# One run of probability products per attention group instead of two, on one Trainium2 core

## The chip, the cores and the metric

The kernel runs on one core of a Trainium2 chip. The metric is the device time of one execution in microseconds (us), taken as the median over several runs. A run is called no different when it lies within 0.2% of the other kernel's time.

## The reference

The reference is an attention layer followed by a small mixture-of-experts layer, for 8 batches of 512 tokens with 512 features:

```python
x = x + attention(layernorm(x), ctx)     # 16 heads of 32, causal mask, softmax
x = x + experts(layernorm(x))            # 8 experts, for each output the two best of 8 logits
```

Only attention is touched by the change. There, with `q = norm(x) Wq`, `k, v = ctx Wkv`, the output of a head is `softmax(q k' / sqrt(32), causal) v`, and the heads' outputs are projected with `Wout` and added to `x`.

## The kernel before

**Groups and steps.** Attention takes the first 615 us or so. A group is four heads of one batch; there are 4 groups a batch (`c` = 0 to 3) and 32 in all (`n`). The loop over a group has 8 steps (`v` = 0 to 7). In step `v` the kernel makes transposed, shifted scores for key block `v // 2` (128 keys) and one pair of the four heads. Key block `kb` holds 512, 384, 256 or 128 columns of queries (causal), so steps 0 and 1 are wide and 6 and 7 narrow.

**Who does what in a step.** TensorE runs two matmuls of `shifted_scores` (L705) into the one PSUM tile `e_ps`. ScalarE takes their exponential into `pT[kb]` (L1095). TensorE may start the next step's L705 only when that exponential has ended. GpSimd then zeroes the masked triangle (`hide_future`, L1836) and, from step 2 on, adds the probabilities of the later key blocks into `acc` (`add`, L1828 and L1823), which is what the sums of the softmax are made from.

**Work for the next group.** The shift of the scores is minus the maximum of each row. TensorE makes the unshifted scores of the group after, three steps ahead (`scores`, L672, in four units of two heads by turns: two PSUM banks, one for each head). VectorE takes their maxima (L1390 and, where masks are added by a matmul, L1384); a bank's next score waits for the maximum of its last. In step 5 TensorE turns the maxima (`turn_maxima`, L687); ScalarE (`hi_shift`, L1020) and VectorE (`lo_shift`, L1399) split them in two parts, and SyncE copies both parts by DMA into two rows of `qk_st` (`rows`, L380, parts `nm_h` and `nm_l`). The next group's first L705 waits for both copies:

```python
if v == 0:
    pe.wait_ge(s["rows_in"], (n + 1) * (16 * SHIFT_ROWS))
```

**Fillers.** The rest of TensorE's work in the steps is put there by tables: queries three groups ahead in steps 0, 2, 3, 4 (`QUERY`), keys in step 5 or 6, values (c = 0 only, steps 0, 2, 3, 4), transposes of tokens (c = 0, steps 6 and 7, `turn_tokens`), and the output projection of the batch before (`project`, 16 steps of a batch: c = 1 steps 0 to 3, 6, 7; c = 2 steps 0, 1, 3 to 6; c = 3 steps 0 to 3). Queries, keys, values and projections are three matmuls of 512 columns each (L261, L262, L263).

**The products with probabilities.** `values_of` (L721) multiplies `v` by `pT[kb]`; `first_sums` (L733) and `other_sums` (L741) multiply ones by `pT[0]` and `acc`. These are matmuls with 32 weight columns, four side by side in the array, while everything else uses all 128 columns (or 16 in L687). The products of key blocks 0 and 1 and the first sums run in step 7 of their own group, those of key blocks 2 and 3 and the other sums in step 1 of the next. In step 2 ScalarE begins the inverse of the sums. The exponential of step 0 of the next group writes `pT[0]` and waits for the products that read it:

```python
if some(n):
    act.wait_ge(s["pv"], (n - 1) * QB + kb + 1)
    act.wait_ge(s["added"], (n - 1) * ADDS + max(v - 1, v % 2 + 1))
```

The last group has a routine of its own (`last_group`), so 31 groups use the code that changes.

Of the kernel before, what the change touches and what calls it, by code (L numbers as in the profile page):

```python
# [27 lines left out]
KC = H // P  # L28
QB = S // P
# [16 lines left out]
def build(nc, x, ctxT, wqT, wkvT, woT, routerT, router_b, expertT, expert_b, out):  # L46
    ctx = ExitStack()
    with ctx:
        def sem(name):
            return ctx.enter_context(nc.semaphore(name))  # L50
# [166 lines left out]
        s = {n: sem(n) for n in names}  # L217

        def some(value):

            return not isinstance(value, int) or value > 0
# [52 lines left out]
        def block_of(v):  # L274

            return QB - 1 - v // 2

        TURN = 5
        LAST = 7
        QUERY = {0: 0, 2: 1, 3: 2, 4: 3}  # L280
        VALUE = {0: 0, 2: 1, 3: 2, 4: 3}
        SUMMED = 1
        STATISTICS = ((2, 0), (2, 1), (3, 0), (3, 1))
        NORMALISED = ((2, 7), (3, 1), (3, 3), (3, 7))
        LAST_GROUP = {3: 0, 5: 1, 7: 2}
# [33 lines left out]
        def out_block(c, v, last):  # L319

            for i, (c0, v0) in enumerate(OUT_FIRST_LAST if last else OUT_FIRST):
                chunk = (c - c0) * UNITS + v - v0
                if 0 <= chunk < KC:
                    return i, chunk
            return None
# [283 lines left out]
        def _(pe):  # L609

            def freed(task, k):
                for name in {"Q": ("q_hi", "q_lo"), "K": ("k_hi", "k_lo"), "V": ("v_ok",),
                             "LNT": ("xT_hi", "xT_lo"), "WO": ("x1_ok",)}[task]:
                    pe.wait_ge(s[name], k + 1)

            def norm_turn(g, i, bank):

                pe.wait_ge(s["xn_ok"], g + 1)
                for k in range(KC):  # L620
                    mm = pe.transpose(j_ps[bank][:, k * P:(k + 1) * P], xt[:, i, k * P:(k + 1) * P], ident[:])
                mm.then_inc(s["xT_mm"], 1)
# [36 lines left out]
            def scores(n, c, v, heads=(0, 1), mask=False):  # L659

                u = n * UNITS + v
                i, pair = block_of(v), v % 2
                w = (i + 1) * P
                if v < 2 and 0 in heads:

                    pe.wait_ge(s[f"stacked{pair}"], (n + 1) * (16 * STACK_DMAS))
                for j in heads:
                    hh = 2 * pair + j

                    if some(2 * u - 1):  # L670
                        pe.wait_ge(s["negmax"], 2 * u - 1 + j)
                    mm = pe.matmul(s_ps[:, j, 0:w], qk_st[c][0:STACK, 0, hh, i * P:w], qk_st[c][0:STACK, 1, hh, 0:w],  # L672
                                   start=True, stop=not mask)
                    if not mask:
                        mm.then_inc(s["scores"], 1)
                if mask:
                    for j in heads:
                        pe.matmul(s_ps[:, j, i * P:w], ident_r[:], mask_r[:], start=False, stop=True)\
                            .then_inc(s["scores"], 1)
# [32 lines left out]
            def values_of(n, c, b, kb):  # L712

                pe.wait_ge(s["causal"], n * UNITS + 2 * kb + 2)
                pe.wait_ge(s["v_ok"], b * QB + kb + 1)
                if kb == 0:
                    if some(n):
                        pe.wait_ge(s["o_ok"], n)
                for hh in range(HC):
                    h = c * HC + hh  # L720
                    mm = pe.matmul(o_ps[hh * HD:(hh + 1) * HD, kb * P:S], v_sb[:, kb, h * HD:(h + 1) * HD],  # L721
                                   pT[kb][:, hh, :], start=(kb == 0), stop=(kb == QB - 1),
                                   tile_position=(0, hh * HD), skip_group_check=True)
                if kb > 0:
                    mm.then_inc(s["pv"], 1)

            def first_sums(n, turned):

                if turned:
                    pe.wait_ge(s["nm_hi"], n + 2)  # L730
                    pe.wait_ge(s["nm_lo"], n + 2)
                for hh in range(HC):
                    mm = pe.matmul(d_ps[hh * HD:(hh + 1) * HD, 0:P], ones[:], pT[0][:, hh, 0:P],  # L733
                                   start=True, stop=True, tile_position=(0, hh * HD), skip_group_check=True)
                mm.then_inc(s["pv"], 1)

            def other_sums(n):

                pe.wait_ge(s["added"], (n + 1) * ADDS)
                for hh in range(HC):  # L740
                    mm = pe.matmul(d_ps[hh * HD:(hh + 1) * HD, P:S], ones[:], acc[:, hh, :],  # L741
                                   start=True, stop=True, tile_position=(0, hh * HD), skip_group_check=True)
                mm.then_inc(s["summed"], 1)
# [16 lines left out]
                                   skip_group_check=True)  # L760
                mm.then_inc(s["summed" if kb == QB - 1 else "pv"], 1)

            def finish_group(n, c, b):
                values_of(n, c, b, QB - 2)
                values_of(n, c, b, QB - 1)
                other_sums(n)

            pe.wait_ge(s["const_one"], 1)
# [38 lines left out]
            def body(b, first, more, further):  # L807
                last = not more
                held = [("K", b * KC + AHEAD - 1), ("Q", b * KC + AHEAD - 1)]

                def take(bank, task, k):
                    freed(*held[bank])
                    held[bank] = (task, k)

                for c in range(KC):
                    n = b * KC + c
                    ahead = more or c == 0

                    def project(v):
                        i, chunk = out_block(c, v, last)  # L820
                        if chunk == 0:
                            take(0, "WO", (b - 1) * QB + i)
                        project_out(b - 1, i, chunk, 0)

                    def turn_tokens(i):
                        take(1 - i % 2, "LNT", (b + 1) * QB + i)
                        norm_turn((b + 1) * QB + i, i, 1 - i % 2)

                    for v in range(UNITS):
                        out = not first and out_block(c, v, last) is not None  # L830
                        final = last and c == KC - 1
                        shifted_scores(n, c, v, final)
                        g, vv = target(c, v - 1)
                        if not masked((c if v else c - 1) % KC, (v - 1) % UNITS) and (more or c + g < KC):
                            scores(n + g, (c + g) % KC, vv, (1,))
                        if c == 1 and v == 0 and out:
                            project(v)
                        if c == 0 and v in VALUE:
                            take(0, "V", b * QB + VALUE[v])
                            values(VALUE[v])  # L840
                        if v in QUERY and ahead:
                            if QUERY[v] == 0:
                                take(1, "Q", n + AHEAD)
                            queries(n + AHEAD, (c + AHEAD) % KC, QUERY[v])
                        if v == SUMMED and not (first and c == 0):
                            finish_group(n - 1, (c - 1) % KC, b if c else b - 1)
                        if final and v in LAST_GROUP:
                            last_group(LAST_GROUP[v])
                        if v == key_step(c) and ahead:
                            take(key_bank(c), "K", n + AHEAD)  # L850
                            keys((c + AHEAD) % KC, b if c == 0 else b + 1, key_bank(c))
                        if v == LAST and not final:
                            values_of(n, c, b, 0)
                            first_sums(n, more or c < KC - 1)
                            values_of(n, c, b, 1)
                        if c == 0 and more:
                            for i in TURNED.get(v, ()):
                                turn_tokens(i)
                        if out and not (c == 1 and v == 0):
                            project(v)  # L860
                        g, vv = target(c, v)
                        if more or c + g < KC:
                            if masked(c, v):
                                scores(n + g, (c + g) % KC, vv, mask=True)
                            else:
                                scores(n + g, (c + g) % KC, vv, (0,))
                        if v == TURN and (more or c < KC - 1):
                            turn_maxima(n + 1, c + 1)
# [1090 lines left out]
```

## Time and profile before

| | |
|---|---|
| median of 3 runs | 1986.51 us (1984.96 to 1989.05) |
| profiled execution, span | 1984.3 us |
| TensorE matmul (PE) busy | 1910.6 us, 96% of the span |
| VectorE (DVE) busy | 1432.1 us, 72% |
| ScalarE (ACT) busy | 1039.0 us, 52% |
| GpSimd (POOL) busy | 850.5 us, 43% |
| chain that ended last | PE 83%, DVE 7%, DMA 3%, issue 2%, POOL 2%, ACT 2% |

A profile comes from one execution, so sums are made against its span. The busy time of PE is that of modelled ends of pipelined matmuls: what tells how long PE is held is the distance from one start to the next. PEld is the loading of weights, which normally lies under the matmul before.

### The profile page before, as it was taken

The page shows a single profiled execution, that of the slowest core. Times are in us where ns is not written, and L with a number is a line of the kernel's source. Part 1 is how long each engine was busy: PE and PEld are TensorE (multiplying, and loading weights), DVE is VectorE, ACT ScalarE, POOL GpSimd, SP SyncE. Part 2 cuts the span into 40 slices and gives each one's busy share as a digit, 9 for nine tenths or more (in the row PEclk, how much of TensorE's full clock was granted, in tenths as well). Part 3 has the DMA queues.
Part 4 walks back from the last instruction along what each step waited for, and adds up shares of the span by engine and source line. Part 5 has one row for each costly group of instructions (what it writes and reads, how often), then busy time and mean ns, then how long its engine had stood idle before and what let it go on. Part 6 is the DMA issues. An engine that isn't in the chain of part 4 may idle for free.

```text
span 1984.3 us, 30426 instructions
## 1 busy us (share of the span) xinstructions
PE 1910.6 (96%) x9772; PEld 1514.7 (76%) x9772; DVE 1432.1 (72%) x2840; ACT 1039.0 (52%) x2062; POOL 850.5 (43%) x1016
## 2 busy tenths in 40 slices
PE   4899999999998999999999999999999999999999
PEld 3666766777765788888888888778888888888887
DVE  5667667767668658787888888477777777777732
ACT  2566566566554347877777787533443333344400
POOL 5577777777674135456445435102321111232100
PEclk8999999999999999999999999999999999999999
DMA  5454555455466468787856555822232222223111
GB/s 166 121 125 130 137 144 128 124 149 134 108 166 229 159 229 274 231 271 221 254 203 217 190 186 196 313 85 79 94 118 85 80 95 85 80 86 124 49 42 33
DMA packets 103693, 294.54 MB, mean 148 GB/s; under 512 B 13777, under 2 KB 14801, under 8 KB 98482
## 3 DMA queue, kind: packets, MB, share of 16 engines
q1 hardware_dynamic: 91394, 209.44, 33.1%
q10 hardware_dynamic: 8880, 67.37, 10.5%
q0 software_dynamic: 3328, 16.78, 3.7%
q8 instruction: 25, 0.41, 0.1%
q14 instruction: 66, 0.54, 0.1%
HBM read 150.31 MB, written 109.16 MB: 131 GB/s over the span
## 4 chain that ended last, share of the span: by engine, by line
PE 83%; DVE 7%; DMA 3%; issue 2%; POOL 2%; ACT 2%; ACTq 0%; SPq 0%; DVEq 0%; POOLq 0%
PE pair L261 20%; PE pair L263 20%; PE pair L262 20%; PE pair L672 3%; PE ps L721 3%; PE ps L261 3%; PE pair L705 3%; PE ps L262 3%; PE ps L263 3%; DMA w_raw<-w_fix 1%; DVE pair L1390 1%; PE ps L741 1%; DVE w_raw L1525 1%; POOL pT L1836 1%; PE ps L902 1%
## 5 line engine op out<-in xcount | busy, mean ns | idle before, releaser
L261 PE MATMUL pair<-w_h,hT 128*128 128x512 f32 x1920 | 751.7, 392 | 6.4 <-ACT w_h L1201 3.6
L263 PE MATMUL pair<-w_h,hT 128*128 128x512 f32 x1920 | 748.5, 390 | 0.0
L262 PE MATMUL pair<-w_l,hT 128*128 128x512 f32 x1920 | 748.3, 390 | 0.0
L1908 POOL TENSOR_TENSOR logits<-logits,second 128x512 f32<-128x512 f32 x224 | 298.6, 1370 | 590.9 <-DVE second L1605 590.6
L261 PEld LDWEIGHTS pair<-w_h,hT 128*128 128x128 f32 x1920 | 361.4, 188 | 81.9 <-issue 5.8
L263 PEld LDWEIGHTS pair<-w_h,hT 128*128 128x128 f32 x1920 | 361.1, 188 | 75.8
L262 PEld LDWEIGHTS pair<-w_l,hT 128*128 128x128 f32 x1920 | 361.3, 188 | 74.1
L1708 DVE SCALAR_TENSOR_TENSOR xb<-pair,c_all,xb 128x512 f32<-128x512 f32 x256 | 191.7, 749 | 195.6 <-PE pair L263 189.5
L1095 ACT ACTIVATE pT<-pair,zero 128x1024 f32<-128x1024 f32 (+3 forms) x256 | 202.6, 792 | 192.0 <-PE pair L705 183.6
L1390 DVE CUSTOM_DVE_ANT_0 pair<-pair,future 128x256 f32<-128x256 f32 (+3 forms) x340 | 184.1, 554 | 124.3 <-PE pair L672 115.9
L1191 ACT ACTIVATE w<-tree 128x512 f32<-128x512 f32 x32 | 20.3, 635 | 388.6 <-DVE tree L1607 388.6
L672 PE MATMUL pair<-qk_st 96*128 96x256 f32 (+3 forms) x512 | 159.3, 341 | 21.7 <-DVE nmax L1390 7.8
L1836 POOL TENSOR_SCALAR_AFFINE_SELECT pT<-pT 128x256 f32<-128x256 f32 x248 | 105.6, 426 | 137.1 <-ACT pT L1095 136.8
L1659 DVE SCALAR_TENSOR_TENSOR scrap<-ps,w 128x512 bf16<-128x512 f32 x224 | 152.9, 683 | 0.8 <-ACT w L1194 0.8
L1170 ACT ACTIVATE over<-over 128x512 f32<-128x512 f32 x224 | 141.7, 633 | 7.0
L1167 ACT ACTIVATE junk<-over 128x512 bf16<-128x512 f32 x224 | 141.5, 632 | 7.1
L1653 DVE SCALAR_TENSOR_TENSOR ps<-logits,ps 128x512 f32<-128x512 f32 x192 | 133.2, 694 | 16.3
L672 PEld LDWEIGHTS pair<-qk_st 96*128 96x128 f32 x512 | 96.8, 192 | 62.9 <-issue 23.9
L705 PE MATMUL pair<-qk_st 98*128 98x256 f32 (+3 forms) x512 | 133.2, 341 | 8.3 <-ACT pT L1095 6.3
L1162 ACT ACTIVATE over<-logits 128x512 f32<-128x512 f32 x224 | 130.2, 624 | 8.6 <-POOL logits L1908 7.6
L1828 POOL TENSOR_TENSOR acc<-acc,pT 128x512 f32<-128x512 f32 (+1 forms) x124 | 125.2, 1010 | 10.3
L1823 POOL TENSOR_TENSOR acc<-pT,pT 128x768 f32<-128x768 f32 x62 | 114.4, 1846 | 5.2
(166 smaller groups left out, 2609.7 us busy)
## 6 DMA issues: line engine op xcount, KB each, us to landing
logits<-lg_all ACTq DMA_DIRECT2D x32, 1792.0 KB, 8.9
qk_st<-qk SPq DMA_DIRECT2D x372, 128.0 KB, 2.4
lg_all<-ev_a SPq DMA_DIRECT2D x31, 768.0 KB, 8.5
lg_all<-ev_b SPq DMA_DIRECT2D x31, 768.0 KB, 3.8
xb<-x SPq DMA_DIRECT2D x64, 256.0 KB, 2.9
hT_all<-hT SPq DMA_DIRECT2D x32, 512.0 KB, 4.3
hT<-hT_all SPq DMA_DIRECT2D x32, 512.0 KB, 4.0
xt<-in_x SPq DMA_DIRECT2D x8, 1024.0 KB, 5.4
```

Of the source, the lines that this page charges most:

```text
L261: pe.matmul(dst, lh, rh, start=start, stop=False)
L262: pe.matmul(dst, lh, rl, start=False, stop=False)
L263: return pe.matmul(dst, ll, rh, start=False, stop=stop)
L672: mm = pe.matmul(s_ps[:, j, 0:w], qk_st[c][0:STACK, 0, hh, i * P:w], qk_st[c][0:STACK, 1, hh, 0:w], start=True, stop=not mask)
L705: mm = pe.matmul(dst[:, j, 0:w], qk_st[c][0:STACK + SHIFT_ROWS, 1, hh, kb * P:(kb + 1) * P], qk_st[c][0:STACK + SHIFT_ROWS, 0, hh, kb * P: ...
L1095: act.activation(pT[kb][:, pair:pair + 2, :], src[:, :, 0:S - kb * P], ACT.Exp, bias=zero[:])\
L1167: act.activation(junk[:], over[j][:], ACT.Sign, accum_out=sign_sum[:, i, e:e + 1])\
L1170: act.activation(over[j][:], over[j][:], ACT.Tanh, scale=0.5, accum_out=tanh_sum[:, i, e:e + 1]).then_inc(s["first_step"], 1)
L1390: dve.tensor_tensor_reduce(row, row, future[:, S - (i + 1) * P:S], -1.0, -MASKED, ALU.add, ALU.min, accum_out=nmax[:, c % 2, at:at + 1]).t ...
L1659: dve.scalar_tensor_tensor(scrap[:, e % 2, :], taken_ps[e % 2], 1.0, w2[:], ALU.min, ALU.mult, accum_out=c_taken[:, i, e - 1:e]).then_inc( ...
L1708: dve.scalar_tensor_tensor(xb[i][:], l_ps[e % 4], c_all[:, t, e:e + 1], xb[i][:], ALU.mult, ALU.add).then_inc(s["acc"], 1)
L1908: pool.tensor_tensor(logits[t % 2][:, e - 1, :], logits[t % 2][:, e - 1, :], second[:], ALU.subtract)\
```

## The change

The run in step 7 and the run in step 1 are taken out. In their place `weigh_values` runs all of it in step 0 of the next group: key block 0, first sums, key blocks 1, 2, 3, other sums. It stands after that step's L705 and the second head's score, ahead of the projection, values and queries. The waits in it are those that the parts had; the number and shape of the matmuls stay the same.

```diff
-        LAST = 7
-        SUMMED = 1
...
-            def first_sums(n, turned):
-
-                if turned:
-                    pe.wait_ge(s["nm_hi"], n + 2)
-                    pe.wait_ge(s["nm_lo"], n + 2)
+            def first_sums(n):
+
+                pe.wait_ge(s["nm_hi"], n + 2)
+                pe.wait_ge(s["nm_lo"], n + 2)
...
-            def finish_group(n, c, b):
-                values_of(n, c, b, QB - 2)
-                values_of(n, c, b, QB - 1)
+            def weigh_values(n, c, b):
+                values_of(n, c, b, 0)
+                first_sums(n)
+                for kb in range(1, QB):
+                    values_of(n, c, b, kb)
                 other_sums(n)
...
+                        if v == 0 and not (first and c == 0):
+                            weigh_values(n - 1, (c - 1) % KC, b if c else b - 1)
                         if c == 1 and v == 0 and out:
                             project(v)
...
-                        if v == SUMMED and not (first and c == 0):
-                            finish_group(n - 1, (c - 1) % KC, b if c else b - 1)
...
-                        if v == LAST and not final:
-                            values_of(n, c, b, 0)
-                            first_sums(n, more or c < KC - 1)
-                            values_of(n, c, b, 1)
```

## Rows read from the trace of the kernel before

**Rows 1.** First line of the page: the span.

```profile
span 1984.3 us, 30426 instructions
```

**Rows 2.** Timeline, PE, from c = 2 step 7: start us, us, what, xcount.

```profile
392.83 0.44 PE L672 MATMUL pair<-qk_st 96*128 96x512 f32 x1
393.20 1.06 PE L721 MATMUL ps<-pT,v_sb 128*32 128x512 f32 x8
...
395.06 0.44 PE L672 MATMUL pair<-qk_st 96*128 96x384 f32 x1
395.35 0.63 PE L705 MATMUL pair<-qk_st 98*128 98x512 f32 x2
...
397.56 0.63 PE L705 MATMUL pair<-qk_st 98*128 98x512 f32 x2
398.02 0.34 PE L672 MATMUL pair<-qk_st 96*128 96x384 f32 x1
398.29 0.86 PE L721 MATMUL ps<-pT,v_sb 128*32 128x256 f32 x16
398.97 0.83 PE L741 MATMUL ps<-acc,ones 128*32 128x384 f32 x8
399.73 0.50 PE L261 MATMUL ps<-wo_h,oT_h 128*128 128x512 f32 x1
400.06 0.39 PE L262 MATMUL ps<-wo_l,oT_h 128*128 128x512 f32 x1
400.29 0.39 PE L263 MATMUL ps<-wo_h,oT_l 128*128 128x512 f32 x1
...
400.64 0.52 PE L705 MATMUL pair<-qk_st 98*128 98x384 f32 x2
```

**Rows 3.** Timeline, SyncE's queue: issues of the second row, c = 1, 2, 3.

```profile
374.62 0.59 SPq L380 DMA_DIRECT2D qk_st<-nm_l  x1
...
392.91 0.59 SPq L380 DMA_DIRECT2D qk_st<-nm_l  x1
...
410.38 0.59 SPq L380 DMA_DIRECT2D qk_st<-nm_l  x1
```

**Rows 4.** Line L380: time to landing, over all groups.

```profile
DMA to landing us min/median/max: 1.8/1.8/3.9
```

**Rows 5.** Line L705: what its engine's idle time ended with, us, times.

```profile
  ACT pT L1095: 24.8, 61
  DMA qk_st<-nm_l: 4.0, 5
```

**Rows 6.** Timeline, ScalarE, step 1 of c = 3.

```profile
398.30 1.12 ACT L1095 ACTIVATE pT<-pair,zero 128x1024 f32<-128x1024 f32 x1 [1.01 <-PE pair L705]
```

**Rows 7.** Timeline, VectorE, c = 0 step 7.

```profile
355.88 1.20 DVE L1384 TENSOR_REDUCE nmax<-pair 128x2 f32<-128x1024 f32 x1
```

**Rows 8.** Timeline, PE: end of c = 0, start of c = 1.

```profile
358.39 0.59 PE L672 MATMUL pair<-qk_st 96*128 96x384 f32 x2
...
360.50 0.47 PE L261 MATMUL ps<-wo_h,oT_h 128*128 128x512 f32 x1 [0.82 <-DVE xnT_l L1360]
```

**Rows 9.** Timeline, PE: first step of c = 2.

```profile
377.79 0.63 PE L705 MATMUL pair<-qk_st 98*128 98x512 f32 x2
```

**Rows 10.** Timeline, PE: first three steps of the next batch's c = 0.

```profile
412.34 0.72 PE L705 MATMUL pair<-qk_st 98*128 98x512 f32 x2
...
414.64 0.63 PE L705 MATMUL pair<-qk_st 98*128 98x512 f32 x2
...
417.04 0.34 PE L705 MATMUL pair<-qk_st 98*128 98x384 f32 x1
```

**Rows 11.** Timeline, GpSimd: last add of the group c = 3.

```profile
414.54 0.74 POOL L1828 TENSOR_TENSOR acc<-acc,pT 128x256 f32<-128x256 f32 x1
```

**Rows 12.** Timeline, PE: steps 1 and 2 of c = 2, first batch.

```profile
92.54 0.73 PE L705 MATMUL pair<-qk_st 98*128 98x512 f32 x2 [0.16 <-ACT pT L1095]
...
95.03 0.51 PE L705 MATMUL pair<-qk_st 98*128 98x384 f32 x2
```

## The prediction

> **What bounds the kernel now.** I read the page first (1984.3 us, [rows 1]), then the timeline of TensorE in the middle batches, then the queues of the engines that it waits for. TensorE holds the chain almost throughout, so a first guess is that only its own time counts. The timeline says otherwise for the places that the change touches. Distances between the first L705 of one step and of the next give the length of a step. At the border from c = 2 to c = 3, step 0 takes 395.35 to 397.56 = 2.21 us and step 1 takes 397.56 to 400.64 = 3.08 [rows 2]. Two things that run beside TensorE are hidden there by the two runs of products:
>
> - In step 7 the rows of the maxima are on their way. The copy of `nm_l` is issued at 392.91 and lands 1.8 us later, at 394.71 [rows 3, 4]; the next group's first L705 starts at 395.35. There are 0.64 us between, and with some 0.09 us for TensorE to restart, 0.55 us of real slack. Already now L705 has waited five times for this copy, 4.0 us in all [rows 5].
> - In step 1 the wide exponential is running. It starts at 398.30 and takes 1.12 [rows 6], so step 2 cannot begin before 399.42, plus 0.05 for the restart: 1.9 us after the step's start at 397.56. The run of products covers all of it.
>
> **The change, part by part.** Per group, in TensorE's starts:
>
> *Switches.* Between matmuls of 128 columns of weights and those of 32, starts lie further apart. Before the run in step 7, a matmul of 512 columns holds TensorE for 0.37 us (392.83 to 393.20), while its normal distance is 0.23 (400.06 to 400.29): 0.14 lost. Before the run in step 1 it is 0.27 (398.02 to 398.29) for 384 columns, whose share of 0.23 is 0.17: 0.10 lost. At the way out, the eight of L741 (3,072 columns) take 0.76 against 0.68 for the sixteen of L721 ahead of them (3,072 columns too): 0.08 lost; and the first full matmul after it takes 0.33 instead of 0.23: 0.10 lost [rows 2]. The two runs themselves are 1.86 (393.20 to 395.06) and 1.44 (398.29 to 399.73), 3.30 together. With the switches, step 7 sheds 0.14 + 1.86 + 0.10 = 2.10, step 1 sheds 0.10 + 1.44 + 0.10 = 1.64, and step 0 gains 3.30 - 0.08 + 0.10 + 0.10 = 3.42; I take 3.40 (the first weights of a run are loaded once less). Alone this would save 2.10 + 1.64 - 3.40 = 0.34 a group, for 31 groups 10.5 us. The Trainium skill ("TensorEngine Tiling (Array Packing)", Key Properties) says that changing the tiling mode drains the engine; it gives no price and speaks for the change, and by it alone the result would be the second rival below.
>
> *Step 7 can't get 2.10 shorter.* The next group's L705 needs the rows, and their chain (maxima, turn, two parts, two copies) begins in step 5 and doesn't contain the products, so it doesn't get shorter. What can be saved is the slack:
> - c = 1 to 2: copy issued 374.62 [rows 3], landed 376.42, restart 376.51, now used at 377.79 [rows 9]: 1.28 saved.
> - c = 2 to 3: 0.55, as above.
> - c = 3 to the next batch: issued 410.38 [rows 3], landed 412.18, restart 412.27, now used at 412.34 [rows 10]: 0.07 saved.
> - c = 0 to 1: here VectorE is later than the rows. Its reduction of two wide maxima ends at 355.88 + 1.20 = 357.08 [rows 7], after which the scores that now start at 358.39 [rows 8] could start at about 357.2: 1.2 saved.
>
> The Trainium skill ("DMA: Bandwidth & Descriptors", Anatomy of one DMA) gives every DMA about 2.0 us of fixed cost. This trace has 1.8 for an 8 KB copy, which decides; by the page's figure, as an estimate, slack would be 0.2 less at c = 1 and c = 2 and the 0.07 gone, 3.7 us more over the kernel.
>
> *Step 1* loses its cover and is then as long as the loop L705, exponential, L705: 1.9 us. It goes from 3.08 to 1.9 for c = 1, 2, 3 (1.18 saved) and, having no projection, from 2.40 (414.64 to 417.04 [rows 10]) to 1.9 for c = 0 (0.50 saved). Of 1.64 shed the rest comes back as a wait.
>
> *Step 0* gains 3.40. The work there isn't short of cover. The exponential of step 0 must now wait for the first part of the run (it reads `pT[0]`), but that is over about 1.1 us into the run; the exponential takes 1.12 [rows 6], while the rest of the run and a query take 2.9. I cost this wait at nothing; without the query 0.6 us of cover would be left. VectorE has no new score for those 3.4 us, which it doesn't miss: its next needed result is the bank of the score at the end of the step. At c = 1, TensorE now waits 0.82 us before the projection, for VectorE's token parts [rows 8]; the run comes before it and hides this: 0.82 saved. GpSimd's last add for c = 3 ends at 414.54 + 0.74 = 415.28 [rows 11]. The merged run would start near 412.27 + 0.73 and want it after the run's 1.78 + 0.68, at 415.46: just in time, so nothing, but with only 0.2 us to spare. Waits of `first_sums` for both parts of the maxima are met before the step begins, since the copies read them. No DMA moves past another in a queue, and inverse and later steps keep their places, so a saving there isn't to be had.
>
> *The sum,* at each border, as step 0 minus what steps 7 and 1 give back:
> - c = 0 to 1: 3.40 - 1.2 - 0.82 - 1.18 = +0.20
> - c = 1 to 2: 3.40 - 1.28 - 1.18 = +0.94
> - c = 2 to 3: 3.40 - 0.55 - 1.18 = +1.67
> - c = 3 to 0: 3.40 - 0.07 - 0.50 = +2.83
>
> Eight times the first three (2.81) are 22.5, seven times the last 19.8, together 42.3 us. The first batch has no projections: its step 1 is 2.49 now (92.54 to 95.03 [rows 12]) and saves 0.59 instead of 1.18, which adds 0.6 at each of three borders, 1.8. I take the last batch like the middle ones. That is +44.1 on a span of 1984.3, or 2028.4; the median of the runs lies 2.2 above the span, so **2030 us**. After attention nothing changes, and the delay is passed on whole.
>
> **The rivals.**
> - *Rows not binding.* If the rows land earlier than TensorE wants them (say, because SyncE's queue gets to them sooner), step 7 may shed up to the 2.10: 0.82 more at c = 1, 1.55 at c = 2, 2.03 at c = 3, in all 8 x 2.37 + 7 x 2.03 = 33 us back, 1997. VectorE's two maxima and the exponential of step 7 would stop it about halfway: 2013. For it: most groups show no wait for the copy today. Against it: the slack is under 1.3 in all three places. Chance 0.10.
> - *Only TensorE's time counts* (the other side): the switches saved, 10.5 us, 1976. It would need the waits of steps 7 and 1 together to stay under 0.34 us a group; by the rows they are 0.3 at the best border and 3 at the worst. For it: TensorE holds the chain. Chance 0.05.
> - *No measurable change:* waits and switches cancel, 1986. They would have to be ten times smaller than read. Chance 0.03.
> - *GpSimd becomes the end of it:* the margin of 0.2 us at c = 3 goes, because masks wait for exponentials that the run delays. Each us that its last add is late costs up to 7 us for seven borders, and the same in the last batch where it has copies to wait for: 2038 to 2045. Chance 0.12.
>
> **How the numbers follow.** The forecast has 0.70. Its own spread is some 8 us (0.3 us for each border's reading): 2022 to 2038. The range of 2010 to 2044 takes in the halfway case and most of the GpSimd case; 1976, 1986 and the tails are left out. Within 0.2% is about what a measurement here can't tell from no change. Slower 0.92, same 0.03, faster 0.05.
>
> **What the new profile would show.** Step 0 of a middle group some 5.6 us long (2.21 + 3.40), with one run L721, L733, L721, L741 in it; step 1 at 1.9 us with its last idle time ended by the exponential L1095; step 7 shorter by 0.1 to 1.3 us, and L705's wait for `nm_l`, now 4.0 us in all, at 20 to 40 us. TensorE's busy time is about the same and its share lower. I am wrong if step 7 comes out under 1.5 us at c = 2, if step 1 does under 1.7, or if the products wait for GpSimd's add in most groups.

## The result and the profile after

| | median | runs | ratio to the kernel before (95%) |
|---|---|---|---|
| before | 1986.51 us | 5 | |
| changed | 2054.54 us (2052.15 to 2056.36) | 5 | 1.0342 (1.0331 to 1.0353) |

The change makes the kernel 68 us slower. I had forecast slower, by 44, and a range that ends at 2044: the direction is right and the size is not. The profiled execution of the changed kernel has a span of 2054.0, 69.7 above [rows 1].

```profile
span 2054.0 us, 30431 instructions
```

**The border c = 2 to 3, as forecast.** This is the timeline of TensorE in the changed kernel at the same border as in [rows 2], one batch earlier: batch 3, counted from 0, where [rows 2] has batch 4. In both kernels batches 1 to 4 agree to within 0.1 us in every step but step 0 of c = 0 (L703 is the former L705, L670 the former L672, L719, L730 and L738 the products; some rows left out):

```profile
351.59 0.34 PE L703 MATMUL pair<-qk_st 98*128 98x128 f32 x2
351.77 0.45 PE L670 MATMUL pair<-qk_st 96*128 96x512 f32 x1
352.61 0.44 PE L670 MATMUL pair<-qk_st 96*128 96x384 f32 x1 [0.39 <-DVE nmax L1385]
353.74 0.73 PE L703 MATMUL pair<-qk_st 98*128 98x512 f32 x2 [0.69 <-DMA qk_st<-nm_l]
...
354.58 1.06 PE L719 MATMUL ps<-pT,v_sb 128*32 128x512 f32 x8
355.46 0.40 PE L730 MATMUL ps<-pT,ones 128*32 128x128 f32 x8
355.68 1.48 PE L719 MATMUL ps<-pT,v_sb 128*32 128x384 f32 x24
356.98 0.83 PE L738 MATMUL ps<-acc,ones 128*32 128x384 f32 x8
357.74 0.50 PE L261 MATMUL ps<-xnT_h,wq_h 128*128 128x512 f32 x1
...
359.40 0.63 PE L703 MATMUL pair<-qk_st 98*128 98x512 f32 x2
...
361.32 0.62 PE L703 MATMUL pair<-qk_st 98*128 98x384 f32 x2 [0.29 <-ACT pT L1090]
```

Read it by the starts of the first L703 of each step. Step 7 is 351.59 to 353.74 = 2.15 us. The wait for VectorE's maximum comes first, and the last idle time ends with the landing of `nm_l`. Step 0 is 5.66 us with the merged run in it, step 1 is 1.92, ended by the exponential. The steps that I had worked out were 2.13 (2.68 less 0.55), 5.6 and 1.9.

**The border c = 3 to the next batch, which is not as forecast.** Same view, one group later (batch 3 to 4); compare [rows 10], which has the border after that:

```profile
370.27 0.44 PE L703 MATMUL pair<-qk_st 98*128 98x128 f32 x2
370.55 0.45 PE L670 MATMUL pair<-qk_st 96*128 96x512 f32 x1
371.80 0.44 PE L670 MATMUL pair<-qk_st 96*128 96x384 f32 x1 [0.80 <-DVE nmax L1385]
373.14 1.22 PE L703 MATMUL pair<-qk_st 98*128 98x512 f32 x2 [0.90 <-DMA qk_st<-nm_l]
374.15 0.53 PE L670 MATMUL pair<-qk_st 96*128 96x384 f32 x1
374.61 1.93 PE L719 MATMUL ps<-pT,v_sb 128*32 128x512 f32 x8
376.32 0.65 PE L730 MATMUL ps<-pT,ones 128*32 128x128 f32 x8
376.74 2.78 PE L719 MATMUL ps<-pT,v_sb 128*32 128x384 f32 x24
379.30 0.99 PE L738 MATMUL ps<-acc,ones 128*32 128x384 f32 x8
...
381.89 0.63 PE L703 MATMUL pair<-qk_st 98*128 98x512 f32 x2
```

Step 7 is 2.87 us (forecast 2.80), but step 0 is 8.75 us instead of 5.7. There is no wait in the run: the eight matmuls of key block 0 hold TensorE for 1.71 us (374.61 to 376.32), against 0.88 (354.58 to 355.46) one group earlier. The same work takes twice the time. The table of stretches of the same kernel says why (columns: stretch, length, busy time of PE, PEld, DVE, ACT, POOL, then the granted clock, the share of DMA and GB/s):

```profile
369.50:373.10 3.60, 1.66 (x5) 0.78 (x5) 3.41 (x12) 2.42 (x5) 3.43 (x5) 0.96 0.02 5
373.10:381.90 8.80, 8.76 (x59) 4.39 (x60) 0.62 (x2) 1.71 (x2) 3.17 (x5) 0.63 0.87 203
373.14:379.65 6.51, 6.51 (x47) 2.96 (x51) 0.62 (x2) 1.11 (x1) 3.13 (x5) 0.50 0.86 200
379.65:381.90 2.25, 2.25 (x16) 1.42 (x9) 0.00 (x0) 0.60 (x1) 0.00 (x0) 1.00 0.92 213
381.90:389.00 7.10, 6.39 (x32) 5.01 (x32) 4.70 (x15) 5.82 (x9) 4.64 (x6) 1.00 0.22 81
```

In the 3.6 us before the merged run TensorE was busy for 1.66. At the end of that stretch, whose mean is 0.96, the granted clock fell: the mean of step 0 is 0.63. Its first 6.51 us are at 0.50 (1.2 GHz), the last 2.25 at 1.00 (2.4 GHz); the two rows of that lie inside the row of the whole step. The step looks perfectly busy (8.76 of 8.80 us), and only the clock column and the distance of starts tell. The lengths of this step in the seven borders are 8.23, 8.53, 8.72, 8.75, 7.16, 7.31 and 8.62 us.

What L703's engine waited for answers to [rows 5]: the rows' copy went from 4.0 us to 45.7, the exponential from 24.8 to 54.2.

```profile
  ACT pT L1090: 54.2, 116
  DMA qk_st<-nm_l: 45.7, 43
```

I had expected 20 to 40 us for the copy. I had also expected TensorE's busy time to stay about the same; it rose from 1910.6 to 1941.6 us with the same 9772 matmuls. So part of the loss is time in which TensorE works slower, not time in which it waits.

### The profile page after: what moved, and what is told of

It reads as the page before. It is cut to its first block, busy times and chain, and to the rows that moved or that the text cites. A ratio compares the mean times of both kernels' runs of the same rounds, so it can differ in the third digit from the quotient of the medians.

```text
span 2054.0 us, 30431 instructions
## 1 busy us (share of the span) xinstructions
PE 1941.6 (95%) x9772; PEld 1523.6 (74%) x9772; DVE 1426.6 (69%) x2840; ACT 1040.3 (51%) x2062; POOL 848.2 (41%) x1016
## 4 chain that ended last, share of the span: by engine, by line
PE 60%; DMA 2%; DVE 2%; ACT 1%; issue 0%; SPq 0%; ACTq 0%; DVEq 0%
PE pair L261 20%; PE pair L263 20%; PE pair L262 20%; DMA w_raw<-w_fix 1%; PE ps L897 1%; DMA xb<-x 1%; DVE w_raw L1520 0%; DVE w_raw L1524 0%; DVE w_l L1561 0%; DMA hT_all<-hT 0%; ACT w_h L1196 0%; ACT w_h L990 0%; ACT ev_c L1219 0%; DVE tree L1579 0%; DVE tree L1580 0%
## 5 line engine op out<-in xcount | busy, mean ns | idle before, releaser
L670 PE MATMUL pair<-qk_st 96*128 96x256 f32 (+3 forms) x512 | 161.5, 346 | 35.0 <-DVE nmax L1385 17.0
L703 PE MATMUL pair<-qk_st 98*128 98x256 f32 (+3 forms) x512 | 140.6, 356 | 39.9 <-DMA qk_st<-nm_l 22.3
L670 PEld LDWEIGHTS pair<-qk_st 96*128 96x128 f32 x512 | 97.5, 194 | 71.2 <-DVE nmax L1385 24.9
L703 PEld LDWEIGHTS pair<-qk_st 98*128 98x128 f32 x512 | 82.4, 194 | 72.3 <-ACT pT L1090 37.0
```

Source lines behind the costliest of these rows:

```text
L703: mm = pe.matmul(dst[:, j, 0:w], qk_st[c][0:STACK + SHIFT_ROWS, 1, hh, kb * P:(kb + 1) * P], qk_st[c][0:STACK + SHIFT_ROWS, 0, hh, kb * P: ...
```

## The experiments

| kernel | median | ratio to before (95%) |
|---|---|---|
| `after_warm` | 2041.33 us | 1.0278 (1.0259 to 1.0298) |
| `seven_to_zero` | 2038.77 | 1.0259 (1.0242 to 1.0276) |
| `one_to_zero` | 2011.82 | 1.0131 (1.0111 to 1.0151) |
| `c3_apart` | 2020.51 | 1.0165 (1.0147 to 1.0183) |
| `after_norows` | 2022.79 | 1.0182 (1.0167 to 1.0198) |
| `before_norows` | 1985.11 | 0.9993 (0.9983 to 1.0002) |
| `late_c0` | 1983.16 | 0.9983 (0.9974 to 0.9992) |
| `late_c0_q1` | 1978.44 | 0.9962 (0.9948 to 0.9976) |
| `after_warm3` | 2051.48 | 1.0329 (1.0310 to 1.0348) |
| `after_warm_more` | 2039.36 | 1.0254 (1.0237 to 1.0272) |

The theory after the result: the two places that I had named (rows and exponential) cost what I had worked out, and the idle time that they leave in step 7 of c = 3 lets the clock fall, so that the merged run behind it goes at half speed. The rival: something inside the merged run holds it up there.

### `after_warm`: TensorE kept at work in step 7 of c = 3

```diff
+                        if v == 7 and c in (3,) and not final:
+                            pe.wait_ge(s["nm_hi"], n + 2)
+                            pe.wait_ge(s["nm_lo"], n + 2)
+                            for _ in range(8):
+                                pe.matmul(d_ps[:, P:S], wq_h[:, 0, 0:P], xnT_h[:, 0, 0:S - P], start=True, stop=True,
+                                          skip_group_check=True)
```

> The changed kernel with eight added matmuls (384 columns each, result unused, not read by anything) in step 7 of the group c = 3, where TensorE otherwise stands idle until the rows land. Theory of the clock: the missing time is the granted clock that falls to 1.2 GHz at the end of c = 3, so that the merged run in step 0 of c = 0 goes at half speed; with TensorE kept at work the clock holds, step 0 of c = 0 falls from some 8.5 to about 5.7 us, and seven borders at 2.5 to 3 us give about 2036. Rival, a wait inside the merged run (GpSimd's last add, or the tiled weights): the filling changes nothing, step 0 of c = 0 stays above 8 us and the time at 2054 or a little more.

Measured: 2041.33. This is "the filled kernel" below. The same border, timeline of TensorE and the table of stretches:

```profile
362.82 0.45 PE L670 MATMUL pair<-qk_st 96*128 96x512 f32 x1
363.12 1.58 PE L855 MATMUL ps<-xnT_h,wq_h 128*128 128x384 f32 x8
...
365.42 0.72 PE L703 MATMUL pair<-qk_st 98*128 98x512 f32 x2 [0.55 <-DMA qk_st<-nm_l]
365.98 0.34 PE L670 MATMUL pair<-qk_st 96*128 96x384 f32 x1
366.25 1.06 PE L719 MATMUL ps<-pT,v_sb 128*32 128x512 f32 x8
367.13 0.40 PE L730 MATMUL ps<-pT,ones 128*32 128x128 f32 x8
```

```profile
362.50:365.40 2.90, 2.34 (x13) 1.96 (x12) 2.67 (x10) 1.70 (x3) 2.82 (x4) 1.00 0.02 6
365.40:371.10 5.70, 5.68 (x59) 3.30 (x60) 0.75 (x4) 1.71 (x2) 3.23 (x5) 1.00 0.87 200
```

The wait for the rows is still there. The added work (L855) costs nothing, and after it the granted clock is 1.00 and step 0 is 5.65 us, in six of the seven borders within 0.05 of that. One, the first, is 6.22. The clock is at 1.00 there as well; the other sums wait for GpSimd's last add (L738 `[0.31 <-POOL acc L1829]`). The rival is out: with nothing changed in the merged run, more work before it makes it take its 5.7 us. By the spans (2054.0 and 2036.8) this is 17.2 us; the medians differ by 13.2. The profiled execution was the fastest of the four of this kernel (2038.59), so the medians are the safer measure.

### `after_warm3`: three matmuls instead of eight

> As the filled kernel, but with three of the unused matmuls instead of eight in step 7 of c = 3: of some 2.1 us that TensorE stands idle there 0.5 are filled instead of 1.4. The rows hold that step anyway, so the matmuls themselves cost nothing in either. Theory of the clock: less filling, more falls, so a time between 2041 and 2054, with the clock at half in the merged run of some batches and not of others. Rival (what helped was something else in the added code, such as its waits for the two parts of the maxima): the same 2041 as with eight.

Measured: 2051.48. Step 0 of c = 0 is 6.21, 5.66, 5.65, 7.34, 8.53, 7.26 and 7.29 us in batches 1 to 7, and the first batch's step 0 of c = 2 is 8.10. Step 0 of c = 3 is at half clock too in batches 5 and 6 (7.30 and 7.35 us), behind a step 7 that has no filling in either kernel. So with 0.5 us of filling the clock holds at some borders and falls at others: at c = 3 to 0 it fell in seven of seven without filling, in four with three matmuls, in none with eight. What helped in the first kernel was the work of the matmuls and not the waits beside them, which are the same here.

### `after_warm_more`: filling in the first and last batch too

```diff
+                        if v == 7 and not final and (c == 3 or (c < 3 if first else last and c == 0)):
...
+                            for _ in range(8):
+                                pe.matmul(d_ps[:, P:S], wo_h[:, 0, 0:P], wo_h[:, 0, 0:S - P], start=True, stop=True,
+                                          skip_group_check=True)
```

> As the filled kernel with eight, and the same eight in step 7 of c = 0, 1, 2 of the first batch and of c = 0 of the last, where the record of the changed kernel has two more merged runs at half clock (6.66 instead of 4.97 us in the first batch, 7.19 instead of about 5 in the last). Theory of the clock: both go, 1.7 + 2.2 us less, and in c = 0 of the first batch, which isn't idle, the eight matmuls cost 1.4: 2039. Rival (the last batch's long step 0 is a wait on something else): that step stays above 7 us, 2041 or more.

The added matmuls read another tile than those of `after_warm` (`wo_h` on both sides) and have the same shape.

Measured: 2039.36. The two steps fall as expected, from 6.66 to 4.97 us in the first batch (step 0 of c = 2) and from 7.19 to 4.79 in the last (step 0 of c = 1). Attention as a whole got 3.0 us shorter by the profiles (624.1 against 627.1, first L703 to the last group's step 7), but the stretch behind it, which has no added matmul, 5.2 longer. It isn't more than 3.0 since in this profile another merged run (c = 3 in batch 5, 7.29 us) was caught at half clock, and the first batch's step 7 of c = 0 got 0.7 us longer. So the record of single steps confirms it; the medians of the two filled kernels can't be told apart.

### `c3_apart`: the border c = 3 to 0 as before

```diff
+        EARLY0 = (0, 1, 2)
+        LATE0 = (0, 1, 2)
...
+                        pc, pb = (c - 1) % KC, b if c else b - 1
+                        if v == 0 and not (first and c == 0):
+                            if pc in EARLY0:
+                                first_part(n - 1, pc, pb)
+                            if pc in LATE0:
+                                second_part(n - 1, pc, pb)
...
+                        if v == 1 and not (first and c == 0) and pc not in LATE0:
+                            second_part(n - 1, pc, pb)
...
+                        if v == 7 and not final and c not in EARLY0:
+                            first_part(n, c, b, more or c < KC - 1)
```

Here `first_part` is key block 0, first sums and key block 1, `second_part` key blocks 2 and 3 and the other sums.

> The change everywhere but at the border c = 3 to the next batch, where the two runs stand in steps 7 and 1 as before. Theory of the clock: the fall comes from the long idle stretch of c = 3 alone; it is gone, the granted clock is 1.00, and what is left is 0, +0.95, +1.7 us at the other three borders, eight times: +21 and some 2 for the first batch, about 2009. Rival, that any of the shortened steps 7 lets the clock fall: falls stay in the record at c = 1 or c = 2, and the time is over 2015.

Measured: 2020.51, above both 2009 and the 2015 that I had set as the rival's mark; the rival held. The seven borders at c = 3 are back at 2.3 and 2.4 us for steps 0 and 1, and the batches 1 to 4 cost 2.9 to 3.0 us each, where the forecast for their three borders was 2.8. But the clock fell elsewhere: step 0 of c = 3 was 7.33 us in batch 5 and 6.66 in the first, and the last batch cost 7.7. Mean granted clock between 60 and 615 us:

```profile
60.00:615.00 555.00, 514.06 (x3449) 366.62 (x3447) 362.93 (x982) 321.09 (x487) 388.84 (x545) 0.98 0.49 127
```

It is 1.00 over the same stretch in the filled kernel and 0.97 in the changed one. So "the long idle stretch of c = 3 alone" was too strong: there it falls every time, behind the step 7 of the other groups sometimes.

### `seven_to_zero` and `one_to_zero`: each half of the change alone

With the scheme of the last diff: `EARLY0 = (0, 1, 2, 3)`, `LATE0 = ()` for the one, and the reverse for the other.

> One part of the change alone: the products of key blocks 0 and 1 and the first sums go from step 7 to step 0, the rest stays in step 1. By the slack in step 7 (1.2, 1.28, 0.55, 0.07 us) against 2.1 us put into step 0, the borders give about 0, +0.8, +1.55, +2.0 us, in all +32 at full clock: 2018. Theory of the clock: step 7 of c = 3 is as idle as in the whole change, so the clock falls again and step 0 (and perhaps 1) of c = 0 is some 2.5 us longer, about 2036. Rival: with step 1 keeping its run the clock holds, 2018.

Measured: 2038.77. In the middle batches step 7 is 2.40, 2.11, 2.13 and 2.87 us long and step 1 keeps its 2.4 and 3.1, as worked out. Step 0 of c = 0 is 5.85 to 6.06 us instead of 4.4: the clock is at 0.72 over it.

```profile
364.90:370.90 6.00, 5.91 (x35) 3.08 (x36) 0.63 (x2) 1.71 (x2) 3.24 (x5) 0.72 0.85 198
```

The time is close to the forecast of 2036 partly by luck: each of these seven steps is 1.5 us too long and not 2.5, and three others, which I hadn't counted, lost 1.6 to 2.9 us to the clock (6.60 us at c = 3 of the first batch, 6.00 at c = 3 of batch 5, 5.91 at c = 1 of the last).

> The other part alone: key blocks 2 and 3 and the other sums go from step 1 to step 0, step 7 keeps its run. Step 7 unchanged, no idle time there, granted clock at 1.00 through attention. Step 0 gains 1.64, step 1 falls to 1.9 us; at the border c = 3 to 0 GpSimd's last add ends 1.5 us after it is wanted, so a wait for it comes in seven times. Borders -0.4, +0.5, +0.5, +2.65: +23, about 2010. Rival without the wait for GpSimd: 2000.

Measured: 2011.82. Timeline of TensorE at the border c = 3 to 0:

```profile
352.48 0.72 PE L705 MATMUL pair<-qk_st 98*128 98x512 f32 x2
...
353.31 0.64 PE L721 MATMUL ps<-pT,v_sb 128*32 128x256 f32 x8
354.65 0.43 PE L721 MATMUL ps<-pT,v_sb 128*32 128x128 f32 x8 [0.70 <-POOL pT L1845]
355.38 0.85 PE L741 MATMUL ps<-acc,ones 128*32 128x384 f32 x8 [0.31 <-POOL acc L1837]
```

The wait for GpSimd's last add was forecast, the one for its mask wasn't; together they have the forecast size (step 0 is 5.38 us, where 2.31 + 1.64 would be 3.95). Step 7 keeps its run, and the clock is at 1.00 in all middle batches. The two halves cost some 52 and 25 us, together 77, against 68 for the whole change, so they don't simply add: this half alone waits for GpSimd's add, the whole change doesn't. Most of the loss, and all of the clock's up to the last group, belongs to the half that empties step 7.

### `after_norows` and `before_norows`: no wait for the rows

```diff
-                if v == 0:
+                if v == 0 and final:
                     pe.wait_ge(s["rows_in"], (n + 1) * (16 * SHIFT_ROWS))
...
-                    mm = pe.matmul(dst[:, j, 0:w], qk_st[c][0:STACK + SHIFT_ROWS, 1, hh, kb * P:(kb + 1) * P],
-                                   qk_st[c][0:STACK + SHIFT_ROWS, 0, hh, kb * P:S], start=True, stop=not final)
+                    mm = pe.matmul(dst[:, j, 0:w], qk_st[c][0:STACK, 1, hh, kb * P:(kb + 1) * P],
+                                   qk_st[c][0:STACK, 0, hh, kb * P:S], start=True, stop=not final)
```

In both kernels ScalarE's exponential is scaled by 0.001 as well, and SyncE still makes the copies.

> The changed kernel without the shift: the shifted scores use 96 rows instead of 98, so L705's successor no longer waits for the copies (they are still made), and the exponential is scaled by 0.001; the softmax is thus computed without its maxima. Theory (step 7 is held by the rows' landing, and that idle time lets the clock fall): step 7 shrinks to what VectorE's maxima allow, about 1.3 us at c = 1 and 2 and 1.8 at c = 3, GpSimd's last add then costs up to 0.9 at c = 3; some 15 us, and with less idle time the clock holds, another 17: about 2022. Rival, VectorE or the exponential holds step 7 anyway: step 7 unchanged, 2050.

Measured: 2022.79. Step 7 is 1.32 us at c = 1, 1.29 at c = 2 and 2.0 at c = 3 (2.12, 2.15 and 2.87 in the changed kernel). At c = 2, in the timeline, what is left of its waits ends with VectorE:

```profile
410.49 0.33 PE L703 MATMUL pair<-qk_st 96*128 96x128 f32 x2
410.66 0.44 PE L670 MATMUL pair<-qk_st 96*128 96x512 f32 x1
411.50 0.44 PE L670 MATMUL pair<-qk_st 96*128 96x384 f32 x1 [0.40 <-DVE nmax L1385]
411.78 0.63 PE L703 MATMUL pair<-qk_st 96*128 96x512 f32 x2
```

So the rows do hold step 7 at c = 1, 2 and 3 in the changed kernel. At c = 0 it stays at 2.40 us: there, as forecast, they don't hold it. The clock I had wrong in part: it still fell in every second batch (step 0 of c = 0 is 7.3 us in four batches), not in none. In the other three it is 6.2 to 6.4 us at full clock, with a wait for GpSimd's last add. That the total meets the forecast is partly luck: between the two profiles all steps 7 together are 22.3 us shorter and all steps 0 12.1, GpSimd's wait included; the forecast had 15 for step 7 and GpSimd together and 17 for the clock.

> The kernel before with the same part left out, as the control: its L705 waits for the copies only 4.0 us in all, so it should gain those at most: 1983 to 1986. Rival: if leaving the rows out changed the exponential or the matmuls themselves, the control would move by more.

Measured: 1985.11, within its interval of no change. The kernel before hardly waits for the rows, and leaving them out, with what goes with it, changes nothing that these runs can tell.

### `late_c0` and `late_c0_q1`: what the change is good for

By the steps above, the one place where a run in step 0 hides something is c = 1, where TensorE waits for VectorE's token parts [rows 8]. `late_c0` is the kernel before with `LATE0 = (0,)`; `late_c0_q1` has besides:

```diff
-                        if v in QUERY and ahead:
-                            if QUERY[v] == 0:
+                        k = {1: 0, 2: 1, 3: 2, 4: 3}.get(v) if c == 1 else QUERY.get(v)
+                        if k is not None and ahead:
+                            if k == 0:
                                 take(1, "Q", n + AHEAD)
-                            queries(n + AHEAD, (c + AHEAD) % KC, QUERY[v])
+                            queries(n + AHEAD, (c + AHEAD) % KC, k)
```

> The kernel before, except that at the border c = 0 to 1 alone the second run (key blocks 2, 3 and other sums) stands in step 0 instead of step 1. By the run with that part moved everywhere: step 0 of c = 1 +0.56 us (the run hides the wait for VectorE's token parts), step 1 -1.18, step 2 +0.12, so -0.5 a batch and -4 us: 1983. Rival: if the wait ahead of the projection only moves on, 1987 or more.

Measured: 1983.16, 0.9983 (0.9974 to 0.9992): 0.5 us less in each of the batches 1 to 5. Its distance to the kernel before is under the 0.2% that counts as a difference here.

> As the last, and at c = 1 the first part of the queries goes from step 0 to step 1, where the exponential leaves TensorE idle for some 0.57 us: step 0 -0.69, step 1 about +0.24 (2.15 us of work against the loop of 1.9), step 2's late start gone: another -0.5 a batch, 1979. Rival: the exponential's loop starts later with the query in it and nothing is saved, as the last run.

Measured: 1978.44, 0.9962 (0.9948 to 0.9976), faster than both kernels. Timeline of TensorE, steps 0 and 1 of c = 1:

```profile
355.72 0.68 PE L705 MATMUL pair<-qk_st 98*128 98x512 f32 x2
356.32 0.86 PE L721 MATMUL ps<-pT,v_sb 128*32 128x256 f32 x16
357.00 0.83 PE L741 MATMUL ps<-acc,ones 128*32 128x384 f32 x8
357.76 0.50 PE L261 MATMUL ps<-wo_h,oT_h 128*128 128x512 f32 x1
...
358.74 0.63 PE L705 MATMUL pair<-qk_st 98*128 98x512 f32 x2
...
359.38 0.39 PE L261 MATMUL ps<-xnT_h,wq_h 128*128 128x512 f32 x1
...
360.88 0.51 PE L705 MATMUL pair<-qk_st 98*128 98x384 f32 x2
```

The run stands where the wait was, and neither it nor the exponential shows as idle time. Steps 0 and 1 take 3.02 and 2.14 us, against 3.15 and 3.10 before, and no step of c = 1 got longer but step 2, by 0.02. That is 1.0 to 1.2 us a batch in batches 1 to 5. Of the 8 us by the medians the two profiles show 5.4 inside attention; the rest lies where nothing was changed.

## Why the prediction was right in direction and wrong in size

Point by point, for steps 7, 0, 1 and 2 around each border, against the kernel before in batch 4. "Full clock" is the filled kernel (`after_warm`), "changed kernel" the one without filling, whose last row is its border from batch 3 to 4 (+4.5 at the border with the shortest step 0, 7.16 us).

| border | forecast | full clock | changed kernel |
|---|---|---|---|
| c = 0 to 1 | +0.20 | 0.00 | -0.03 |
| c = 1 to 2 | +0.94 | +1.12 | +1.08 |
| c = 2 to 3 | +1.67 | +1.88 | +1.88 |
| c = 3 to 0 | +2.83 | +2.97 | +6.1 |

- **The rows' slack in step 7** was right: 1.28, 0.53 and 0.0 us saved at c = 1, 2 and 3, forecast 1.28, 0.55 and 0.07. The experiment without rows shows that they are the cause, so that rival is out as well. At c = 0, where VectorE holds the step, it was 1.23, forecast 1.2. The section that the prediction cites for 2.0 us of fixed cost, the Trainium skill's "DMA: Bandwidth & Descriptors", Anatomy of one DMA, gives that figure for copies issued by way of GpSimd. These are issued by SyncE, and the trace's 1.8 us is what counts for them.
- **Step 1 at 1.9 us** was right (1.91 to 1.92). Left out was that the first matmul after such a wait also loads its weights in the open. In the changed kernel L703 and its weight load both start at 361.32 and the two L703 hold TensorE for 0.45 us (to 361.77). Before, the weight load of L705 starts 0.11 us ahead of the matmul (400.53 and 400.64), and the two hold it for 0.36 (to 401.00). That is 0.1 us in step 2 at each border, some 3 us in all. I had put 0.05 us for the restart.
- **Step 0 plus 3.40** was right where the clock is full: 3.35 to 3.47. At c = 1 it was 2.28 where I had 3.40 less 0.82 = 2.58: the wait that the run hides had been 1.0 between starts, and about 0.1 remains open. With the 0.1 of the restart in step 2 this brings the border to 0.00 instead of +0.20.
- **GpSimd** was right: in the changed kernel L738 never waits for its add. The margin was as thin as forecast, though: at full clock, in `after_warm`, the first border from c = 3 to 0 does wait for it (6.22 us instead of 5.66). With half the change, where TensorE comes earlier, all of them do.
- **The last batch** I had taken like the middle ones. It cost 14.4 us instead of 5.6. Of the 8.8 over, about 3 are its own step 0 of c = 0 at half clock and 2.4 the merged run at c = 1. Another 1.6 are steps 5 and 6 of c = 1, 4.29 us with the clock at 0.50 for 3.4 of them, against 2.74 in `after_warm_more`, where it held. The rest, under 2 us, I haven't traced.
- **The step that failed** is in the sum: "That is +44.1 on a span of 1984.3". Every term of it was TensorE's time at the distances of the kernel before, where the granted clock is 1.00 through the middle batches. I turned work into idle time in step 7 (some 2 us of the 2.9 at c = 3) and didn't ask what idle time does to the price of the work behind it: the sum has no term for the clock, and no reason is given for leaving it out. The clock's share, from the changed kernel's steps: the seven steps 0 of c = 0 sum to 57.3 us against 7 x 5.66 = 39.6, 17.7 too many; the first batch's step 0 of c = 2 is 1.7 over, the last batch's step 0 of c = 1 2.4. That is 21.8 us (0.6 less if the first border is taken at the 6.22 us that it has at full clock), and with 1.6 in the last batch 23.4. The 3 us of restarts come on top. The miss on the spans is 69.7 - 44.1 = 25.6, but that these sums meet it so closely is in part chance. From the first L705 to the last group's step 7 the profiles differ by 72.3 us (643.1 against 570.8), 28.2 over the forecast. Outside that stretch the changed kernel's profile is 0.7 us longer at the start and 3.4 shorter at the end. The end is the same in all kernels, and their profiles range from 1354.7 to 1359.9 us there.

Why the loss is worst at c = 3 can be seen there: that group's steps 6 and 7 have neither a projection nor keys, and TensorE waits for VectorE in both (0.39 us in step 6, not shown; 0.80 in step 7) before it waits for the rows. There the merged run comes behind the longest stretch with little work.

What stays open: why the clock falls at some borders and not at others with the same steps (7.16 us in batch 5, 8.75 in batch 4; three matmuls of filling saved three of seven). The runs show that less idle time makes it rarer: at c = 3 to 0 seven falls in the changed kernel, four with three matmuls or without the rows, none with eight matmuls. They don't show where the limit lies.

## What to carry to other kernels

- A filler is worth what it covers at its place. Before matmuls are gathered to save switches (here 0.34 us a group), ask at both places that lose them which chain runs beside: 2.10 us taken out of step 7 gave back 0.0 to 1.3 us.
- Where a move turns work into idle time on TensorE, price the work behind it at both clocks. A stretch that looks fully busy in the profile can be at half clock, so read the granted clock and the distance of starts together.
- Half of the move (the run of step 1) at the one place that had a real wait (c = 1), with a query moved into the gap that it opens, gave 8 us by the medians, 5.4 of them inside attention by the profiles.

## What the runs showed of the hardware

- Going from matmuls of 128 weight columns to those of 32 cost 0.10 to 0.14 us between starts at full clock, coming back 0.08 + 0.10. Worked out with these, the merged run was to add 3.40 us to step 0, and at full clock it added 3.35 to 3.47.
- At the border c = 3 to 0 in the middle batches the granted clock fell from 2.4 to 1.2 GHz although TensorE was never idle there for longer than 0.9 us at once by the timeline's idle times. In the batch shown it had 1.66 us of work in the 3.6 ahead of the merged run. With the added matmuls there it stayed at 1.00 in the same place. In the first and last batch the idle times ahead of a fall were longer (1.4 and 1.7 us). The Trainium skill ("TensorE: Matmul & The Clock Gate", Part 1: The HAM clock gate) says that a block that watches how busy the engine has been sets the clock. The trace agrees with that reading.
- Matmuls whose results nobody reads, placed where TensorE waits anyway, made the changed kernel 13 us faster by the medians.
